# First q tiles placed on the chip through 64-row staging tiles, loads held behind them, low halves of probabilities on GpSimd, token rows of the second batch by DMA

## The reference

```python
xn = layernorm(x)
q, k, v = split(xn @ Wqkv)                       # q: 32 heads x 16, k and v: 16
scores = q . k * 16**-0.5 + slope[h] * (pos_k - pos_q), masked where pos_k > pos_q
x = x + (softmax(scores) @ v) @ Wo + lora_top2(xn; A, B, Wr)
xn = layernorm(x)
q, k, v = xn . Wq + bq, xn . Wk + bk, xn . Wv + bv   # per token: 16 x 32, 16, 16
p = softmax over e of (sum over heads of q[d]) * k[e] * 16**-0.5
h = silu(xn @ gate_w.T * gate_s) * (xn @ up_w.T * up_s)
x = x + repeat(p @ v, 32) + h @ down_w.T * down_s
```

## Time and profile before

| | us |
|---|---|
| median of 3 runs | 625.92 (625.88 to 626.74) |
| span of the profiled execution, first to last instruction | 623.2 |
| PE busy | 570.7 (92% of the span) |
| DVE busy | 461.3 (74%) |
| ACT busy | 377.0 (61%) |
| POOL busy | 351.7 (56%) |

### The profile page before, as it was taken

One profiled execution on the slowest core, in us unless ns is written; L12 is line 12 of the kernel. 1 busy time (PEld: TensorE's weight loads), 2 busy tenths in 40 slices (PEclk: granted clock), 3 DMA queues, 4 the chain that ended last, 5 costly groups with the idle time before them and its releaser, 6 DMA issues.

```text
span 623.2 us, 14286 instructions
## 1 busy us (share of the span) xinstructions
PE 570.7 (92%) x5590; PEld 421.3 (68%) x5590; DVE 461.3 (74%) x1034; ACT 377.0 (61%) x703; POOL 351.7 (56%) x364
## 2 busy tenths in 40 slices
PE   4579583699999999999999999999999999999997
PEld 4466451467885668776968587858685876785783
DVE  4769874899999874899697748996986569354642
ACT  3287095847875478675757485858684776651240
POOL 6231595724655667674837574848576677542140
PEclk9987895599999999999999999999999999999999
DMA  8767799905054146001610160016001000000000
GB/s 207 152 95 78 123 237 217 170 2 54 2 54 87 37 68 70 3 4 35 88 17 5 35 86 4 4 35 88 1 5 52 18 1 9 28 2 2 35 1 34
DMA packets 98942, 34.97 MB, mean 56 GB/s; under 512 B 75548, under 2 KB 90044, under 8 KB 98876
## 3 DMA queue, kind: packets, MB, share of 16 engines
q1 hardware_dynamic: 76044, 24.58, 22.7%
q0 software_dynamic: 2352, 7.18, 5.7%
q10 hardware_dynamic: 20480, 2.31, 2.6%
HBM read 30.19 MB, written 8.39 MB: 62 GB/s over the span
## 4 chain that ended last, share of the span: by engine, by line
PE 68%; DVE 13%; SPq 8%; ACT 4%; issue 3%; DMA 2%; POOL 2%; ACTq 1%; DVEq 0%
PE B_bank L1266 27%; PE B_bank L1287 14%; PE A_bank L1218 7%; SPq L693 5%; PE A_bank L1191 4%; DVE mx L1537 4%; PE A_bank L1120 3%; PE E_bank L1176 3%; PE B_bank L1154 3%; PE E_bank L1171 2%; PE B_bank L1254 1%; DMA qq<-nmp 1%; ACTq L693 1%; SPq L731 1%; SPq L717 1%
## 5 line engine op out<-in xcount | busy, mean ns | idle before, releaser
L883 POOL TENSOR_TENSOR probs<-e,probs 128x512 f16<-128x512 f32 x176 | 208.3, 1188 | 127.2 <-ACT probs L999 126.8
L1266 PE MATMUL B_bank<-xs,wgu 128*128 128x256 f16 x1792 | 204.3, 273 | 0.3 <-DVE hf L1649 0.3
L998 ACT ACTIVATE e<-E_bank,wn 128x512 f32<-128x512 f32 x192 | 133.7, 696 | 103.4 <-PE E_bank L1176 53.9
L1266 PEld LDWEIGHTS B_bank<-xs,wgu 128*128 128x128 f16 x1792 | 172.7, 98 | 21.6 <-DVE hf L1649 0.6
L999 ACT ACTIVATE probs<-E_bank,wn 128x512 f16<-128x512 f32 x192 | 134.0, 698 | 0.0
L1287 PE MATMUL B_bank<-wd,hbuf 128*128 128x512 f16 x448 | 99.9, 379 | 0.1
L897 POOL TENSOR_TENSOR hbuf<-hf,hbuf 128x512 f16<-128x512 f32 x56 | 65.8, 1176 | 56.2 <-ACT hbuf L1033 55.8
L1537 DVE TENSOR_REDUCE mx<-B_bank 128x2 f32<-128x384 f32 (+5 forms) x168 | 92.1, 603 | 4.5 <-PE B_bank L1154 4.4
L1639 DVE SCALAR_TENSOR_TENSOR hf<-ebuf,B_bank 128x512 f32<-128x512 f32 x56 | 38.3, 684 | 62.2 <-ACT ebuf L1043 61.9
L1287 PEld LDWEIGHTS B_bank<-wd,hbuf 128*128 128x128 f16 x448 | 43.2, 98 | 49.3 <-POOL hbuf L897 0.6
L1043 ACT ACTIVATE ebuf<-B_bank,sgx 128x256 f32<-128x256 f32 x112 | 47.5, 485 | 22.1 <-PE B_bank L1266 20.8
(11 more groups left out here) (199 smaller groups left out, 696.3 us busy)
## 6 DMA issues: line engine op xcount, KB each, us to landing
qq<-q_parts SPq DMA_DIRECT2D x21, 256.0 KB
x<-in_x SPq DMA_DIRECT2D x20, 256.0 KB, 3.1
out_y<-x SPq DMA_DIRECT2D x16, 256.0 KB, 2.0
xa<-in_x SPq DMA_DIRECT2D x12, 256.0 KB, 5.1
q_parts<-qs SPq DMA_DIRECT2D x48, 64.0 KB, 2.9
wgu<-in_gate_w POOLq DMA_DIRECT2D x4, 448.0 KB, 9.1
wgu<-in_up_w POOLq DMA_DIRECT2D x4, 448.0 KB, 8.7
wd<-in_down_w POOLq DMA_DIRECT2D x4, 448.0 KB, 7.1
```

The costliest lines, as they stand in the source:

```text
L883: pool.tensor_tensor(probs[:, u % PSLOTS, 1, :], e32[:, w, :], probs[:, u % PSLOTS, 0, :], ALU.subtract).then_inc(s_lop, 1)
L998: act.activation(e32[:, w, :], psum("exp", i, g, w)[:, :], ACT.Exp, scale=wn[:, 7:8])
L1266: mm = pe.matmul(psum(name, u, i)[:, a * SEQ:(a + 1) * SEQ].rearrange("p (t n) -> p t n", t=NU), wgu[:, m, k, (2 * i + a) * P:(2 * i + a + ...
```

## The change

- **First q on the chip.** `store`, `gather_first` and the first `gather` go. Each q tile of the first chunk is placed by three DMAs of SP (`place`), 128 rows of 512 bytes each, into a staging tile `natural[m]` of 64 rows, in the order head and token; DVE then copies the tile into `qq` in the order block, head and token. The ALiBi rows come into the staging tile by small DMAs (`tables`), the other rows are zeroed by DVE (`zero`), so that one copy fills rows 0 to 63. The second batch reuses the staging tiles.
- **Maxima of the first batch.** They are made in 32 groups of two, in the order of the q tiles (`FIRST_MAXG`), and turned in two halves (`nm0`). They aren't written into `qq`: for batch 0 each score product is followed by products with `pick` (one column for each group, spread over 128) that add the negated maxima in PSUM.
- **Low halves.** `LOWS = 0`: all of them on POOL.
- **Token rows.** DVE makes the one-hot rows of the first batch alone; a DMA (`hot_copy`) copies them for the second.
- **Loads that wait.** x of the second chunk is loaded after the placing of batch 0, Wo after that of batch 1; the FFN loads and `late` wait for the last copy of batch 1 (`s_placed`). `gate(0, 0)` waits for the eight gate and up loads alone, `half(0, 0)` for the others.
- **Smaller edits.** The slope and position tables are scaled on ACT and read in 512-byte runs; the mask and the key constants are loaded between the tiles of x; the float16 identity is made from the float32 one; `clear` goes; wtok's halves are made first (`HI_ORDER`); ACT calls an exponential once at the start (`warm`). The planner's times and ranks are new throughout, so the order of steps changes on all engines.

The core of the diff; the new times and ranks, and the plain renamings, are left out.

```diff
-LOWS = 2
+LOWS = 0
...
+FIRST_MAXG = [(tb, 2 * n, 2) for n in range(NK) for tb in range(NTB)]
+HI_ORDER = [NK, 0, 1, 2, 3] + list(range(NK + 1, 2 * NK + 2))
...
+def groups_of(i):
+
+    return MAXG if i else FIRST_MAXG
...
-    p.add("SP", ("x_load", c), *([pe("q", c - 1, NK - 1)] if c > 1 else [sp("wo", gap=0.0)] if c else []))
+    p.add("SP", ("x_load", c), *([pe("q", c - 1, NK - 1)] if c > 1 else [sp("place", 0, NK - 1, gap=0.0)] if c else []))
...
-        p.add("SP", ("wo",), sp("consts", gap=0.0))
+        p.add("SP", ("wo",), sp("place", 1, NK - 1, gap=0.0))
...
-        p.add("ACT", ("store", b, m), dve("q0", b, m))
+        p.add("SP", ("place", b, m), dve("q0", b, m), *([] if b else [sp("tables", gap=0.0)]), *([dve("place", 0, m)] if b else []))
+        p.add("DVE", ("place", b, m), sp("place", b, m, gap=2.5))
...
-            first += [pool("ffn_load", N_FFN - 1, gap=10.0)]
+            first += [pool("ffn_load", 2 * NK - 1, gap=40.0)]
...
     for n in range(N_FFN):
-        p.add("POOL", ("ffn_load", n), sp("gather", 1, gap=8.0), at=34.0 + 5.0 * n)
+        p.add("POOL", ("ffn_load", n), *([dve("place", 1, NK - 1)] if n == 0 else [pool("late", 8)] if n >= 2 * NK else []))
...
+        natural = [wd[:, NB * NK:NB * NK + NK, :].rearrange("p i n -> p (i n)"), hf[:, :, :].rearrange("p a n -> p (a n)").bitcast(F16),
+                   attnT[:, :, :, :].rearrange("p a k t -> p (a k t)"), x1[:, NT:XSLOTS, :].rearrange("p a n -> p (a n)").bitcast(F16)]
...
             def tables():
-                sp.wait_ge(s_init, 4)
-                for b in range(NB):
-                    zero_rows(b, R_NM, R_HOT).then_inc(s_zero, 16)
+                sp.wait_ge(s_zero, NK)
                 sp.wait_ge(s_pos, 1)
-                for r0, rows in ((R_ALIBI, slope_up), (R_ALIBI + 3, pos_half)):
-                    for b in range(NB):
-                        sp.dma_start(qq[r0:r0 + 3, b, :, :, :].rearrange("a c h t -> a c (h t)"), rows).then_inc(s_posq, 16)
+                for m in range(NK):
+                    for r0, rows in ((R_ALIBI, slope_up), (R_ALIBI + 3, pos_half)):
+                        sp.dma_start(natural[m][r0:r0 + 3, :], rows[m:3 * NK:NK, :]).then_inc(s_natural[m], 16)
+
+            def hot_copy():
+                sp.wait_ge(s_hot[0], NTB * GT // R_HOT)
+                sp.dma_start(qq[R_HOT:P, 1, :, :, :], qq[R_HOT:P, 0, :, :, :]).then_inc(s_hot[1], 16)
...
-            def gather_first(m):
-                gather_heads(sp, 0, (m,), PART_Q, 0)
+            def place(b, m):
+                if b:
+                    sp.wait_ge(s_placed, m + 1)
+                for g, part in enumerate(PART_Q):
+                    if part == 0:
+                        sp.wait_ge(s_q0h, b * NK + m + 1)
+                    else:
+                        wait_used(sp, "q0", b, m)
+                    sp.dma_start(natural[m][g * HD:(g + 1) * HD, :].rearrange("d (h t) -> d h t", t=SEQ),
+                                 q_first[:, b, m, part, :]).then_inc(s_natural[m], 16)
...
                 if n == 0:
-                    pool.wait_ge(s_gather[1], 16 * 3)
+                    pool.wait_ge(s_placed, 2 * NK)
...
-            def store(b, m):
-                wait_used(act, "q0", b, m)
-                store_heads(act, 0, b, m, q_first[:, b, m, :, :], s_q0[b][m])
...
+            def nm0(b, h):
+                wait_full(act, "nm0", b, h)
+                act.activation(nm_first[0:NG // 2, h, :], psum("nm0", b, h)[0:NG // 2, 0:P], ACT.Copy, scale=-1.0 / NM).then_inc(s_nm0, 1)
...
+            def nm0(b, h):
+                wait_used(pe, "max", 0, 2 * NTB * (h + 1) - 1)
+                wait_free(pe, "nm0", b, h)
+                pe.transpose(psum("nm0", b, h)[0:NG // 2, 0:P], mx[:, 0, h * NG // 2:(h + 1) * NG // 2], identf[:, :])\
+                  .then_inc(full("nm0", b, h), 1)
...
+                if i == 0 and g % (NHG // 2) == 0 and w == 0:
+                    wait_used(pe, "nm0", 0, g // (NHG // 2))
+                if i and g == 0 and w == 0:
+                    pe.wait_ge(s_nmrow[b], 32 * (c + b))
...
+                    for c1 in range(0 if i else blocks):
+                        row = g // 2 % 2 * 2 * NTB + 2 * (t0 + c1) + g % 2
+                        mm = pe.matmul(acc[:, c0 + c1, :, :], pick[:, row:row + 1].broadcast_to([NG, P]),
+                                       nm_first[:, g // (NHG // 2), :].rearrange("r (h t) -> r h t", t=GT), start=False, stop=True,
+                                       skip_group_check=True)
...
-                        pe.wait_ge(s_ffn, 16 * N_FFN)
+                        pe.wait_ge(s_ffn, 16 * 2 * NK)
...
+            def zero():
+                for m in range(NK):
+                    dve.memset(natural[m][R_ZERO:R_HOT, :].bitcast(F32), 0.0).then_inc(s_zero, 1)
...
+            def place(b, m):
+                dve.wait_ge(s_natural[m], 32 + 48 * (b + 1))
+                dve.tensor_copy(qq[0:R_HOT, b, :, 8 * m:8 * m + 8, :],
+                                natural[m][0:R_HOT, :].rearrange("d (h c t) -> d c h t", c=NTB, t=GT)).then_inc(s_placed, 1)
```

More of the change, by code:

```diff
@@ L413, in plan @@
         if c == 0:
[L414 removed]
             for m in range(NK):
[L416 removed]
+                p.add("POOL", ("turn", m), at=10.5 + m)
             for m in range(NK):
[L418 removed]
+                p.add("ACT", ("squares", m), at=11.5 + m)
             p.add("PE", ("norm",), act("squares", NK - 1))
```

340 lines of the change are left out of this document (176 added, 164 removed), and 23 rows, old and new, of tables (RANK, US).

## The result

The changed kernel took 656.26 us (median of 4, 651.83 to 657.61) against 626.12 for the kernel before on the same chip: a ratio of 1.0468 (95% interval 1.0434 to 1.0502), 30 us slower where 23 faster were forecast. Its profiled span is 654.5 us.

What follows compares the result with a forecast made beforehand. Other engines pace a 125 us start-up, then PE bounds 498 us. First exponential 41, attention to 84, stall 15, DVE 3: seam 102 against 125.2, 23 less; span 600, time 603 us, range 586 to 618.

Steps and rivals of the forecast that it cites:

- seam: End of the first batch's attention, its output's second transposition, where start-up gives way to gapless PE: 102 against 125.2 us.
- first exponential: In the start-up on ACT: first q kept on chip and halved maxima let it start near 41 us, not 77.8.
- length of the first attention, to its last division: After the first exponential: 41 us of ACT work plus 2 for last products and divisions, ending at 84 us.
- stall and DVE's share behind it, to the second turn: ACT waits 15 us for the second chunk's q stores, placed at 58 to 74 us; DVE adds 3.
- from the turn to a full PE, and what is left then: Behind the seam: PE streams at once, with 498 us left to the end.
- three signs: Forecast wrong if first exponential starts after 50 us, ACT has no hole, or PE idles over 10 us behind the seam.
- PE gapless behind the seam: After the first attention: PE runs without holes for the 498 us to the end.
- Rival F: Second chunk's q stores under the weight stream: one piece passes per weight packet; seam 110, time 611 us, chance 0.05.
- Rival D: All 16 q stores are slowed, third chunk's x lands after 102.5, delaying divisions; seam 139, time 640 us, chance 0.08.
- Low halves on POOL: First two attentions: eight more per batch, 9.1 us each batch, fit in POOL's idle time and cost nothing.
- The `pick` matmuls: First attention on PE: 96 more matmuls, 6 to 14 us, taken as 6, covered by 45 us of PE idle time.
- The 9 us that I left out for placing copies held by POOL: DVE's eight placing copies: possibly each held for one POOL instruction, 9 us together; not in the sum.

Runs made afterwards that it cites:

- e4: Changed kernel with SP's copy of the token rows, x of the second chunk and the output weights issued ahead of the first placing; 650.32 us, ratio 1.0392.
- e16: e13 with x of the second chunk, output weights and normalization of x ahead of tables, masks and zeroing; 636.81 us, ratio 1.0187.
- e1: Changed kernel with only the second batch's row maxima written ahead of the second chunk's query; 647.64 us, ratio 1.0357.
- e9: Changed kernel with e4's early loads and the second chunk's query among the maxima and first units of the first attention; 654.12 us, ratio 1.0468.
- e5: Changed kernel with four staging slots for the second chunk's query in place of two; 652.73 us, ratio 1.0451.
- e3: Changed kernel with thirteen weight loads issued earlier, one ahead of each of POOL's low halves from 70 us on; 650.11 us, ratio 1.0374.
- e7: Kernel before with the sixteen low halves that DVE did in the first two attentions put on POOL; 627.92 us, ratio 1.0034.
- e6: Changed kernel without the 96 matmuls that subtract the first attention's row maxima; 648.93 us, ratio 1.0377.
- e14: e13 without the 96 matmuls that subtract the first attention's maxima; 632.19 us, ratio 1.0103.
- e13: Changed kernel with the edits of e1, e3 and e4 together; 636.34 us, ratio 1.0176.
- e15: e13 with six units of the second attention directly behind the first batch's turns; 638.03 us, ratio 1.0210.
- e17: e13 with the edits of e15 and e16, and the query weights' scaling moved behind the first query tiles; 639.72 us, ratio 1.0247.
- e10: e9 with e1's edit and six units of the second attention directly behind the first; 656.17 us, ratio 1.0501.
- e12: Kernel before with its weight loads spread over POOL's low halves and the set-up steps needing them later; 636.56 us, ratio 1.0173.
- e18: Kernel before with weight loads later than in e12, gate and up weights first, and the second batch's maxima ahead of x1's loads; 631.50 us, ratio 1.0086.

## Why the prediction was wrong

The sum gave a seam at 102 and a span of 600; the span is 654.5. Its terms against the rows:

| term | forecast | measured | off by |
|---|---|---|---|
| first exponential | 41 | 69.06 | +28.1 |
| length of the first attention, to its last division | 43 | 47.6 | +4.6 |
| stall and DVE's share behind it, to the second turn | 18 | 16.8 | -1.2 |
| from the turn to a full PE, and what is left then | 498 | 29.6 + 491.5 | +23.1 |

Two of the three signs that I had named for being wrong came: the first exponential after 50, and more than 10 us of PE idle behind the seam (13.3 from the second turn to 163).

**"The first exponential starts near 41 in place of 77.8" failed.** Of its 28 us, 6.5 are the first tile's low half (31.2 in place of 24.7): zeroing, token rows and masks stand ahead of half the normalization on DVE, and ACT waits for the table rows ahead of the squares. 3.2 and then 7.4 more are the copies: DVE's order has the third tile's low half ahead of the first copy, ACT scales weights before it evicts that tile (36.10), and all four copies come ahead of the first maximum. 10.3 are the first half of the maxima up to its subtraction (47.29 to 67.13, against 9.5), 7.61 of them one wait for a placing DMA that had been issued behind 1 MB of x and 1 MB of token rows. I had priced the steps by when their data is ready; each engine keeps its written order, and I put nothing down for what that order sets ahead. What this term is worth at the end is less: e4 took 4 to 6 us off it and 4.8 off the time, e16 two more for nothing.

**"PE gapless behind the seam" failed**, and it is the larger lesson, because the end hangs on it directly. The seam was defined as the second turn of the first attention. In the kernel before, the second batch's maxima had landed by then; here they are on ACT's, DVE's and SP's lists behind four query tiles and their stores, so PE idles for 13.3 of the 29.6 us behind the turn. e1, which only moves them, gives 6.9 us back.

**The stall was sized rightly and placed wrongly.** 11.3 us of slot waits on ACT (2.66 and 8.65) against 15, but at 112 to 132, not at 58 to 74, since chunk 2's query stands behind the first attention in every list. Moving it forward did not win it back: e9 does so and is 4.8 us slower than e4 alone, but there the query tiles wait for slots inside the first attention, so this does not clear the place. The slot itself is not the loss: e5 took the wait away and SP's queue held x of chunk 3, the gather and the maxima just as long. What pays there is to take the weight stream out of the way of SP's stores (e3, 5.9 us).

**Rival F was thrown out on a wrong reading.** I took 23.66 us of issue for the time in which one tile's 256 pieces per engine pass, and so saw 2.6 pieces for each weight packet. The queue's packets, in a stretch in which both queues have work, say otherwise; kernel before from 77 to 83 us, changed kernel from 122 to 127 (packets, MB, share of 16 engines):

```profile
q0 software_dynamic: 393, 1.24, 104.0%
q1 hardware_dynamic: 393, 0.03, 9.7%
```
```profile
q0 software_dynamic: 329, 1.05, 105.8%
q1 hardware_dynamic: 329, 0.02, 9.3%
```

One for one, exactly: 393 and 393, 329 and 329. A 64-byte piece waits for a weight packet that takes some 0.25 us (16 engines times 6 us times 1.04, over 393), and in these stretches a store of 1024 pieces advances only as fast as the stream has packets. The Trainium skill, "DMA: Bandwidth & Descriptors", section "Queues, rings and completion order", states that an engine goes round its queues packet by packet. The traces agree on the turns; where the page puts some 9 to 17 descriptors into a packet, each 64-byte piece is a packet of its own here. The row that I set against it measured issue, not passage. Between 127 and 132, with 72 weight packets left, 6108 pieces went.

**Rival D (slower) came nearest.** Its condition, x of chunk 3 later than 102.5, is met by 30 us (132.19), and its seam of 139 is 133.41. But D let that x delay DVE's divisions; here they were over at 116.63, and the gap came from the maxima and the gather on SP.

**The parts that I costed at nothing.** Low halves on POOL: 2.1 us (e7, on the kernel before). The `pick` matmuls: 13.9 us busy, more than the 6 that I took and inside the bound of 14; the cover that I named, PE's idle time, is gone by then (busy for 45.1 of the 46 us from 67 to 113), and they cost 5.7 (e6) and 4.6 us (e14). Token rows and x behind the placing: 4.8 (e4). The 9 us that I left out for placing copies held by POOL did not come: the eight took 0.68 us each, but POOL ran no low half beside any of them.

**What stays open.** e13 and e14 account for 22.8 of the 29.3 us. Of the 6.4 that remain I know only that they are not the order of the front or of the second attention's first units as tried (e15 to e17). The low halves may be part of them: their 2.1 us were measured on the kernel before and not on top of e14. Whether the moved query would pay in an order better than mine (e9, e10) is not settled.

## What to carry over

In a kernel whose engines keep a written order, a removed wait is worth what the next steps in each list allow: before pricing it, go down every list that the steps share and ask what was written between them. Define the end of a start-up by the condition under which the bound engine runs full, all its inputs, not by the last step that happened to come before it in one trace. A bulk stream that overlaps small-piece DMAs slows whatever meets it packet for packet, so moving the stream moves the wait: it should meet something that is covered (in the kernel before, the stores are; the maxima in e12 and the set-up in e18 were not).

## What the runs showed of the hardware

- Issue on SP's queue can be held by what is queued: twelve stores of 64 KB took 19.71 us beside the weight stream, one of them 9.79, and 8.65 with the stream ahead of them (e3); three placings of 64 KB went from 1.83 to 5.65 us behind 1 MB of x and 1 MB of token rows. A long stretch of issues need not be this: the 30.61 us of x1's loads were 28.0 us of waiting for DVE.
- The granted TensorE clock stayed low behind a hole: after a stretch from 50 to 60 us with 1.72 us busy, PE ran at 0.50, 1.2 GHz, from 60 to 80, though it was busy for 7.86 and 10 us of the two windows; two `pick` matmuls then took 0.39 us, 0.28 at the higher level. In e9 it read 0.50 from 110 to 130 too, with 9.64 and 9.71 of 10 us busy. What this level cost at the end no run separates.
